# A decoder layer on one core: denominators of the cross-attention groups moved to the third quarter, and both ends rearranged

## What is computed

```python
x = x + attn(layernorm(x), w_qkv, b_qkv, w_dense, b_dense)              # causal, 16 heads of 32
x = x + xattn(layernorm(x), ctx, ctx, mask, Wq, bq, Wk, bk, Wv, bv, Wo, bo)
x = x + ffn(layernorm(x), Wg, bg, W1, b1, W2, b2)                       # argmax of 8 experts, gelu
# inside each attention
scores = einsum('bhqd,bhkd->bhqk', q, k) / sqrt(32)                     # masked
probs  = softmax(scores)
ctx    = einsum('bhqk,bhkd->bhqd', probs, v)
```

## Time and profile before

| What | Value |
|---|---|
| three runs | 1976.71, 1986.3, 1979.91 us; median 1979.91 |
| profiled execution, its own time | 1983.32 us |
| its span, and mean granted clock of PE | 1981.5 us, 0.978 |
| PE, DVE, ACT, POOL busy in the span | 1888.0, 1345.2, 1128.2, 971.7 us |
| cross-attention, 1000 to 1200 us: PE, DVE, ACT, POOL busy | 199.67, 133.37, 112.95, 101.50 us |
| the last attention group, 1575.5 to 1595.5 us: PE busy, granted clock | 17.81 us, 0.50 |
| start of the expert layer | 1613.73 us |

### The profile page before, as it was taken

One profiled execution on the slowest core, in us unless ns is written; L12 is line 12 of the kernel. 1 busy time (PEld: TensorE's weight loads), 2 busy tenths in 40 slices (PEclk: granted clock), 3 DMA queues, 4 the chain that ended last, 5 costly groups with the idle time before them and its releaser, 6 DMA issues. The chain is left out here.

```text
span 1981.5 us, 34914 instructions
## 1 busy us (share of the span) xinstructions
PE 1888.0 (95%) x10950; PEld 1327.1 (67%) x10950; DVE 1345.2 (68%) x2845; ACT 1128.2 (57%) x2164; POOL 971.7 (49%) x1144
## 2 busy tenths in 40 slices
PE   6899999999999999999999999999999875899997
PEld 4667777777777766666666666666666354798896
DVE  5567667676766676667675757576766357688886
ACT  3555555555555555555565556555655434677885
POOL 3445545545554555455554444555454433345553
PEclk9999999999999999999999999999999776999999
DMA  5454554645455574544344545445343446722220
GB/s 165 114 164 108 135 137 97 143 115 123 108 133 134 129 191 91 139 110 110 103 113 102 128 108 126 110 108 118 88 100 80 102 166 192 286 73 92 83 88 16
DMA packets 137659, 239.18 MB, mean 121 GB/s; under 512 B 31067, under 2 KB 32387, under 8 KB 137441
## 3 DMA queue, kind: packets, MB, share of 16 engines
q1 hardware_dynamic: 109184, 191.28, 35.5%
q0 software_dynamic: 21392, 45.37, 11.6%
q10 hardware_dynamic: 6928, 0.63, 0.2%
HBM read 114.84 MB, written 48.97 MB: 83 GB/s over the span
## 5 line engine op out<-in xcount | busy, mean ns | idle before, releaser
L543 ACT ACTIVATE attn_probs<-attn_sT 128x512 f32<-128x512 f32 (+3 forms) x1024 | 528.8, 518 | 475.8 <-PE attn_sT L840 472.4
L451 POOL TENSOR_TENSOR attn_probs<-attn_probs 128x512 f32<-128x512 f32 (+2 forms) x384 | 529.9, 1399 | 174.6 <-PE attn_o_ps L855 128.1
L648 DVE TENSOR_REDUCE attn_m_col<-attn_sS 128x1 f32<-128x512 f32 x512 | 342.6, 688 | 191.1 <-PE attn_sS L824 183.2
L840 PE MATMUL attn_sT<-attn_stack 98*128 98x512 f32 (+2 forms) x1024 | 389.4, 392 | 2.2 <-ACT attn_probs L543 2.2
L824 PE MATMUL attn_sS<-attn_stack 97*128 97x512 f32 (+2 forms) x1024 | 368.7, 370 | 12.6 <-DVE attn_m_col L648 3.2
L654 DVE CUSTOM_DVE_ANT_0 attn_sS<-attn_sS,attn_cT_low 128x128 f32<-128x128 f32 x496 | 241.2, 504 | 170.3 <-PE attn_sS L824 166.5
L840 PEld LDWEIGHTS attn_sT<-attn_stack 98*128 98x128 f32 x1024 | 189.0, 190 | 212.8 <-ACT attn_probs L543 135.1
L439 POOL TENSOR_SCALAR_AFFINE_SELECT attn_probs<-attn_probs 128x256 f32<-128x256 f32 x256 | 119.6, 468 | 350.8 <-ACT attn_probs L543 350.7
L855 PE MATMUL attn_o_ps<-attn_probs,attn_V 128*32 128x512 f32 (+3 forms) x2048 | 236.3, 533 | 6.1 <-ACT attn_probs L543 3.3
L824 PEld LDWEIGHTS attn_sS<-attn_stack 97*128 97x128 f32 x1024 | 193.5, 190 | 67.9 <-DVE attn_m_col L648 15.6
L804 PE MATMUL attn_pj<-attn_xT_high,attn_w_high 128*128 128x512 f32 x384 | 155.0, 404 | 2.6 <-DVE attn_xT_low L632 1.4
(11 more groups left out here) (198 smaller groups left out, 3689.4 us busy)
## 6 DMA issues: line engine op xcount, KB each, us to landing
attn_stack<-attn_stage SPq DMA_DIRECT2D x672, 128.0 KB, 2.3
attn_rows<-in_x_dram SPq DMA_DIRECT2D x64, 256.0 KB, 4.0
attn_rows<-x_after_self SPq DMA_DIRECT2D x64, 256.0 KB, 4.3
moe_w<-in_L_ffn_W_dram SPq DMA_DIRECT2D x16, 1024.0 KB, 15.0
attn_stack<-attn_stage POOLq DMA_DIRECT2D x96, 128.0 KB, 3.3
x_after_self<-attn_rows SPq DMA_DIRECT2D x32, 256.0 KB, 2.6
...
```

Source lines behind the costliest of these rows:

```text
L451: pool.tensor_tensor(total, total, tile_of(n, kb)[:, js, q0:S], ALU.add).then_inc(added, 1)
L543: act.activation(tile_of(n, kb)[:, j, q0:S], sT[:, i % 2, q0:S], ACT.Exp, scale=SCALE).then_inc(exp_done, 1)
L648: dve.tensor_reduce(to, sS[:, k % 2], AX_X, ALU.max).then_inc(s_free, 1)
L840: pe.matmul(sT[:, i % 2, q0:S], stack[0:ROW_MAX + 1, n % 2, 1, j, kb * P:(kb + 1) * P], stack[0:ROW_MAX + 1, n % 2, 0, j, q0:S], start=Tru ...
```

## The change

Five things change.

- **Denominators of late groups.** A late group is a cross group other than the first of its batch (`late`). There POOL adds the fourth key block to the sum tile as well, in two adds of 128x1024 at steps 14 and 15 (the second behind the stack head), and `sums` has only the four products with the sum tile. It runs at the end of step 3 of the next group instead of step 0 (`sums_q`). ACT takes the logarithm at step 4 and the inverse at step 5, DVE the three operations at steps 6 and 7.
- **Correction within PSUM**, in all groups: residual (extra times rec), then `correct_inverse` (extra becomes (extra + 2) times rec), then `divide` (o_sb times extra), at steps 2, 3, 4, or 6, 7, 7 behind a late group.
- **The start.** The first rows are normalised before the weights are split; the split goes in nine pieces, first the q and k columns of the four parts, then their v columns, then the dense weights; the heads 1 and 3 of group 0 are stacked by ACT's queue.
- **The end of attention.** The output of the last batch gets four banks of its own (both pj, both sS). Its chunks 0 to 2 are computed in steps 1 to 15 of group 63, only the four last chunks after the last group's output is split. The bias is added to the rows from step 12 of group 63. In group 63 the output of group 62 is split at steps 6 and 7.
- **The start of the expert layer.** POOL's memset of the row buffers moves behind the fourth batch's layernorm.

```diff
@@ -56,3 +56,3 @@
         what, of, t = (("v", b, 3), ("wo", b - 1, 1), ("wo", b - 1, 3), ("v", b + 1, 1))[g]
-        return (what, of, t) if in_batch(of) else None
+        return (what, of, t) if in_batch(of) and (what, of) != ("wo", NB_ALL - 1) else None
@@ -92,4 +92,10 @@
+    def late(n):
+        return is_cross(n) and n % G != 0
+
+    def sums_q(n):
+        return 3 if late(n) else 0
+
     def adds_before(n):
-        return 6 * n
+        return 6 * n + 2 * sum(late(m) for m in range(n))
@@ -127,3 +133,3 @@
             aux.append(turned_aux(n, q))
-        if q == 0 and in_groups(n - 1):
+        if q == sums_q(n - 1) and in_groups(n - 1):
             aux.append(("den", n - 1))
@@ -260,2 +267,4 @@
         tri_at = [flat.bitcast(BF16) for flat in (cT[1][:, 0, S // 2:S], rows[:, RING - 1, 0:S // 2])]
+        LAST_CHUNKS = {(NG - 1, q): (i % NB, i // NB) for i, q in enumerate((1, 2, 3, 4, 5, 6, 7, 8, 9, 11, 13, 15))}
+        last_bank = [pj[:, 0], pj[:, 1], sS[:, 0], sS[:, 1]]
         N_CONST = 15
@@ -321,2 +330,12 @@
+        N_SPLIT = 2 * KT + 1
+
+        def split_views(i):
+            if i == 2 * KT:
+                _, _, to, of = weight_views(KT)
+                return KT, to, of
+            _, _, to, of = weight_views(i % KT)
+            what = slice(0, 2) if i < KT else slice(2, 3)
+            return i % KT, [w[:, what] for w in to], of[:, what]
+
         def raw_dst(raw, src):
@@ -387,3 +406,3 @@
                 m, j = n + 2, q - J * (NB - 1)
-                if j >= 0 and in_groups(m) and not (is_cross(m) and j == POOL_HEAD):
+                if j >= 0 and in_groups(m) and not (is_cross(m) and j == POOL_HEAD) and not (m == 0 and j % 2):
                     wait_to_stack(sp, m, j)
@@ -404,2 +423,4 @@
             for t in range(NB):
+                store_row(LAST, t)
+            for t in range(NB):
                 sp.wait_ge(stored[t], 16 * NB_ALL)
@@ -449,2 +470,4 @@
                     pool.wait_ge(added, adds_before(n) + j1)
+                if kb == 3:
+                    pool.wait_ge(added, adds_before(n) + J + j1 // 2)
                 total = tile_of(n, 0)[:, js, q0:S]
@@ -453,3 +476,3 @@
             adds_at = {False: {6: ((1, 0, 1),), 8: ((1, 1, 2),), 10: ((1, 2, 3),), 11: ((1, 3, 4),), 12: ((2, 0, 2), (2, 2, 4))},
-                       True: {8: ((1, 0, 1), (1, 1, 2), (1, 2, 3), (1, 3, 4)), 12: ((2, 0, 2), (2, 2, 4))}}
+                       True: {8: ((1, 0, 1), (1, 1, 2), (1, 2, 3), (1, 3, 4)), 12: ((2, 0, 2), (2, 2, 4)), 14: ((3, 0, 2),), 15: ((3, 2, 4),)}}
@@ -481,5 +504,6 @@
                     stack_head(pool, n + 2, POOL_HEAD)
-                if in_groups(n) and q in adds_at[is_cross(n)]:
-                    for part in adds_at[is_cross(n)][q]:
-                        add_probs(n, *part)
+                if in_groups(n):
+                    for part in adds_at[is_cross(n)].get(q, ()):
+                        if part[0] < 3 or late(n):
+                            add_probs(n, *part)
                 u = finished(n - 1, 14) if q == 6 else finished(n, 0) if q == 7 else None
@@ -495,4 +519,4 @@
             def high_of_weights(i):
-                act.wait_ge(raw_loaded[i], 16)
-                _, _, (high, _), raw = weight_views(i)
+                part, (high, _), raw = split_views(i)
+                act.wait_ge(raw_loaded[part], 16)
                 act.copy(high, raw).then_inc(raw_high, 1)
@@ -571,3 +595,2 @@
-            high_of_weights(0)
             for t in range(NB):
@@ -575,4 +598,6 @@
             for n, q in steps:
+                if (n, q) == (-3, 14):
+                    high_of_weights(0)
                 if (n, q) == (-2, 1):
-                    for i in range(1, len(weights)):
+                    for i in range(1, N_SPLIT):
                         high_of_weights(i)
@@ -581,5 +606,6 @@
                     act.wait_ge(const_step, N_STEP)
-                    act.wait_ge(raw_done, len(weights))
+                    act.wait_ge(raw_done, N_SPLIT)
                 if q == 0 and in_groups(n - 1):
                     copy_output(n - 1)
+                if q == 0 and in_groups(n - 1) and not late(n - 1):
                     log_of_sums(n - 1)
@@ -587,3 +613,5 @@
                     exponent(n, q // J, q % J)
-                if q == 0 and in_groups(n - 1):
+                if q == 4 and in_groups(n - 1) and late(n - 1):
+                    log_of_sums(n - 1)
+                if q == (5 if late(n - 1) else 0) and in_groups(n - 1):
                     inverse_of_sums(n - 1)
@@ -599,2 +627,5 @@
                         high_of_rows(t)
+                if n == -2 and q in (13, 15):
+                    wait_to_stack(act, 0, q - 12)
+                    stack_head(act, 0, q - 12)
                 if q == 14 and in_groups(n + 1):
@@ -603,3 +634,3 @@
                                   m_neg[:].bitcast(F32)).then_inc(max_stacked, 16)
-                if q == (14 if n % G == 2 else 12) and in_groups(n - 1):
+                if q == (6 if n == NG - 1 else 14 if n % G == 2 else 12) and in_groups(n - 1):
                     high_of_output(n - 1)
@@ -669,12 +700,11 @@
+            def correct_inverse(n):
+                dve.wait_ge(refined, n + 1)
+                dve.scalar_tensor_tensor(out=extra[:], in0=extra[:], scalar=2.0, in1=rec[:], op0=ALU.add,
+                                         op1=ALU.mult).then_inc(o_scaled, 1)
+
             def divide(n):
                 dve.wait_ge(o_copied, n + 1)
-                dve.wait_ge(inverse_done, 2 * n + 2)
-                dve.tensor_tensor(o_sb[:], o_sb[:], rec[:], ALU.mult).then_inc(o_scaled, 1)
-
-            def refine(n):
-                dve.wait_ge(refined, n + 1)
                 dve.wait_ge(o_scaled, n + 1)
-                dve.scalar_tensor_tensor(out=o_sb[:], in0=extra[:], scalar=2.0, in1=o_sb[:], op0=ALU.add,
-                                         op1=ALU.mult).then_inc(o_divided, 1)
+                dve.tensor_tensor(o_sb[:], extra[:], o_sb[:], ALU.mult).then_inc(o_divided, 1)
                 dve.wait_ge(o_divided, n + 1)
@@ -688,2 +718,14 @@
+            def add_last_bias(t):
+                to = row_block(("r", LAST, t))
+                wait_row(dve, ("r", LAST, t))
+                wait_row(dve, BIAS_AT)
+                dve.tensor_tensor(to, to, row_block(BIAS_AT), ALU.add).then_inc(last_biased, 1)
+
+            def add_last_rows(t):
+                to = row_block(("r", LAST, t))
+                dve.wait_ge(last_biased, t + 1)
+                dve.wait_ge(last_full, t + 1)
+                dve.tensor_tensor(to, last_bank[t], to, ALU.add).then_inc(summed, 1)
+
             def add_rows(u):
@@ -692,6 +734,2 @@
                 wait_row(dve, ("r", b, t))
-                if b == LAST:
-                    wait_row(dve, BIAS_AT)
-                    dve.tensor_tensor(to, to, row_block(BIAS_AT), ALU.add).then_inc(last_biased, 1)
-                    dve.wait_ge(last_biased, t + 1)
                 wait_unit(dve, u)
@@ -708,6 +746,7 @@
                 row_stats(0, t)
-            low_of_weights(0)
             for n, q in steps:
+                if (n, q) == (-3, 15):
+                    low_of_weights(0)
                 if (n, q) == (-2, 1):
-                    for i in range(1, KT):
+                    for i in range(1, 2 * KT):
                         low_of_weights(i)
@@ -729,8 +768,8 @@
                         maximum(key)
-                if q == 2 and in_groups(n - 1):
-                    divide(n - 1)
-                if q == 3 and in_groups(n - 1):
+                if q == (6 if late(n - 1) else 2) and in_groups(n - 1):
                     residual_of_inverse(n - 1)
-                if q == 4 and in_groups(n - 1):
-                    refine(n - 1)
+                if q == (7 if late(n - 1) else 3) and in_groups(n - 1):
+                    correct_inverse(n - 1)
+                if q == (7 if late(n - 1) else 4) and in_groups(n - 1):
+                    divide(n - 1)
                 u = finished(n, q)
@@ -743,3 +782,3 @@
                     negate_max(n + 1)
-                if q == (15 if n % G == 2 else 13) and in_groups(n - 1):
+                if q == (7 if n == NG - 1 else 15 if n % G == 2 else 13) and in_groups(n - 1):
                     low_of_output(n - 1)
@@ -752,2 +791,6 @@
                     low_of_swap(*swap_at[before])
+                if n == NG - 1 and q >= NB * (J - 1):
+                    add_last_bias(q - NB * (J - 1))
+            for t in range(NB):
+                add_last_rows(t)
@@ -795,3 +838,3 @@
                     else:
-                        pe.wait_ge(raw_done, len(weights) if what == "wo" else 1 if u == units[0] else KT)
+                        pe.wait_ge(raw_done, N_SPLIT if what == "wo" else 2 * KT if what == "v" else 1 if u == units[0] else KT)
                 elif u == units[0]:
@@ -863,4 +906,4 @@
                 for j in range(J):
```

(30 more changed lines are left out.)

7 lines of the change are left out of this document (4 added, 3 removed).

## The result

The changed kernel takes 1974.55 us (median of 22 runs, 1968.54 to 1978.33), the kernel before 1977.82 (22 runs, 1973.18 to 1986.3): ratio 0.9976, 95% interval 0.9967 to 0.9986. That is 3.3 us by the medians and 2.8 to 6.5 by the interval, not the 16.4 forecast, and the time lies just above the range's upper end of 1974. One execution of the kernel before, in the series of E9 to E12, took 2320 us at a clock of 0.749; it is left out of every figure.

What follows compares the result with a forecast made beforehand. PE's own instructions bound the middle, the chain both ends; -10.7 + 2.1 - 3.0 - 0.3 - 4.5 = -16.4 us, from the median 1979.91 to 1963.5 us, range 1953 to 1974.

Steps and rivals of the forecast that it cites:

- Part 1: Late groups: two denominator sets leave the end (-1.71), one lone set comes (+1.20); -0.51 us each, -10.7 over 21.
- larger-gain rival: Late groups: a lone set costs only 0.87 us and DVE keeps up; about -27 in all, 1953 us; 13%.
- Part 2: Other engines in late groups: POOL's adds and ACT 0; DVE's three operations at steps 6 and 7 +2.1 us.
- POOL late for the sums: Next group's sums: POOL ready with 2.5 us to spare in the middle; in the last group some 1.6 us later.
- Part 4: End of attention: -0.3 us up to the denominators and -4.5 from the last oT to the last row sum.
- term for 12 products instead of 39: After the last oT: 12 products remain instead of 39; -3.7 to -6.2 us, taken as -4.5.
- Part 3: Start: ACT's split behind normalising and narrower low parts on DVE; -3.0 us, bounds -1.5 and -4.5.
- The memset: Expert layer's start: moving POOL's memset costs 0 to +2.4 us among the row statistics; taken as 0.
- Bunching: DVE's operations at steps 6 and 7 hold back score banks: +8 us (4%) or 27 more, slower (5%); 9%.
- port rival: Late groups: the output's low part on DVE held 1.5 us more, on PE's path; +31, 1995 us, slower; 4%.

Runs made afterwards that it cites:

- E9: Kernel before with the load of row block 2 moved from step 15 to step 13 of the batch's second group; 1977.36 us, ratio 0.9985.
- E12: Changed kernel with the edits of E7 and E8, and groups 62 and 63 not late; 1950.96 us, ratio 0.9860.
- E7: Changed kernel with the load of row block 2 moved from step 15 to step 13 of the batch's second group; 1965.12 us, ratio 0.9934.
- E10: Changed kernel with the edits of E7 and E8 together; 1957.02 us, ratio 0.9881.
- E2: Changed kernel with no group late, both ends and the correction within PSUM kept; 1970.02 us, ratio 0.9958.
- E1: Changed kernel run again without any edit, for a second profile; 1974.44 us, ratio 0.9978.
- E3: Changed kernel with DVE taking both maxima of step 0 ahead of the row sum; 1970.83 us, ratio 0.9963.
- E4: Changed kernel with group 63 not late; 1968.95 us, ratio 0.9954.
- E6: Changed kernel with groups 62 and 63 not late; 1967.44 us, ratio 0.9943.
- E8: Changed kernel with DVE's correction at step 8 and division at step 10 instead of 7, last group excepted; 1965.62 us, ratio 0.9932.
- E11: Changed kernel with the edits of E7 and E8, and group 63 not late; 1952.88 us, ratio 0.9865.

## Why the prediction was wrong, step by step

**What bounds it: held.** PE in the middle, the chain at the ends.

**Part 1, -10.7: held.** Away from the row waits a step takes nearly the same time in group after group, so the steps can be compared one by one. This is the third group of a batch, mean of seven, in us from one transposed score to the next:

| steps | before | E7 | E10 |
|---|---|---|---|
| 3 and 4 (the lone set) | 2.96 | 4.15 | 4.15 |
| 7 | 1.31 | 1.17 | 1.16 |
| 9 and 10 | 2.68 | 3.04 | 2.68 |
| 15 (the group's end) | 4.88 | 3.17 | 3.17 |
| all 16 | 25.39 | 25.07 | 24.71 |

The lone set costs 1.18 us, where I had 1.20, and the end gets 1.72 shorter, where I had 1.71: -0.54 a group, -11.3 in all. So the larger-gain rival's 0.87 for a lone set did not come. In E7, group 46:

```profile
1123.38 0.39 PE L867 MATMUL attn_sS<-attn_stack 97*128 97x512 f32 x1
1123.70 1.06 PE L907 MATMUL attn_extra<-attn_probs,attn_ones 128*32 128x512 f32 x8
1124.69 0.50 PE L883 MATMUL attn_sT<-attn_stack 98*128 98x512 f32 x1
```

**Part 2, DVE +2.1: mis-sized on both sides.** Steps 9 and 10 cost 0.38 us more a late group, 8.0 in all, where I took 0.1 (E10, with the operations apart, takes them back to the old length). The step that failed was the picture of the three operations "laid in one by one" against idle time on one side: steps 6 and 7 put two of them in a row ahead of maxima that were already due. What I put at nothing was the place that they leave: in the kernel before PE waited at step 7 for maxima held back by the same three operations at steps 2 to 4, and that wait is gone, 0.17 us a group, 3.7 in all. (In E2, where the operations are back at steps 2 to 4, step 7 takes 1.33 us again.) Group 46 before, at step 7, and in E7, at steps 9 and 10:

```profile
1136.03 0.19 PEld L824 LDWEIGHTS attn_sS<-attn_stack 97*128 97x128 f32 x1 [0.32 <-DVE attn_m_col L648]
```
```profile
1133.16 0.19 PEld L867 LDWEIGHTS attn_sS<-attn_stack 97*128 97x128 f32 x1 [0.39 <-DVE attn_m_col L679]
...
1133.76 0.19 PEld L867 LDWEIGHTS attn_sS<-attn_stack 97*128 97x128 f32 x1 [0.30 <-DVE attn_m_col L679]
```
A clean batch so came out 1.0 us shorter, where I had 1.2. E10 is 15.8 us shorter than the kernel before between groups 33 and 61, more than part 1 forecast, because the wait at step 7 is gone too, not because the sets cost less. The middle adds up: -11.3 for the sets, +8.0 at steps 9 and 10, -3.7 at step 7, -0.7 in small pieces, +5.0 for the rows below make -2.7, as measured.

**Part 2, what was not in the sum: the row.** This is one of the two steps that made the miss. I looked at what the moved work does to POOL's stack heads and bias loads, and saw DVE's row wait in group 62 only; that a shorter group makes SP's row load late for the third group of the other batches too stood at nothing, without a reason. The load and the heads ahead of it keep their time against the products of the group's end, but the group's end is 1.71 us shorter; so the row, which before landed 0.2 to 1.0 us ahead of the next group's start, now lands 0.4 to 0.7 after it, and in groups 42 and 54 3.3 and 1.6 after it. DVE's wait in all is the same as before, 15.6 us against 15.2, and now it is on PE's path. E7 prices it: 5.0 us between groups 33 and 61, and 9.3 by the medians with group 62, where the kernel before had that wait as well. Why it is just groups 42 and 54 stays open: ahead of group 42 one issue of a stack head took 1.3 to 1.9 us instead of 0.59 in each of six profiles with late sums and the load in its old place (after, E1, E3, E4, E6, E8), and the load 3.6 to 5.4 us to land, where in group 46 it took 2.9 to 3.6.

**POOL late for the sums: right in the middle,** where no product of L907 waited. **At the end** the wait was foreseen and priced at +1.6 us from the start of the group; it came to +2.7 (26.2 against 23.5). Of the 1.1 more, 0.9 are the last four adds, 10.42 us for four instead of 4 x 2.38, beside DVE's four bias additions, 7.96 us for four:

```profile
1572.44 7.96 DVE L723 TENSOR_TENSOR attn_rows<-attn_rows 128x512 f32<-128x512 f32 x4
```
```profile
1574.47 10.42 POOL L474 TENSOR_TENSOR attn_probs<-attn_probs 128x1024 f32<-128x1024 f32 x4 [0.82 <-ACT attn_probs L567]
```

**Part 4, -4.8: right against the wrong base,** the other step that made the miss. From group 61 to the last row sum the two profiles after are 4.0 and 3.4 us shorter than the one I worked from. But in that one the last group was at half clock; in three of five it is not, and against those (86.5) the changed kernel is 1.6 us slower: groups 61 and 62 take 1.8 us less, the last group 9.3 us more up to its denominators, and what follows 5.9 us less. I read the 0.50 of the earlier trace rows as what the kernel does, took its length as the thing to beat, and put the result on the median of all executions. The profiled execution's 3.4 us above the median could have warned me. The term for 12 products instead of 39, -4.5, held against its own base: from the last oT to the last row sum 5.48 us after, 9.94 before. There was luck in it: in the three profiles with a full-clock last group the same stretch took 11.5 us, 6.1 more than after.

**Part 3, -3.0: held** within what the profiles differ: 776.9 on average over the eleven profiles with the new start in the table, 779.7 over the six of the kernel before. The first score starts 4.0 us sooner on average, where I had 3. The memset I set at 0 within 0 to 2.4: the rest of the span is 1.0 us longer on average, 371.7 (E11 left out) against 370.7. Neither the start nor the memset was tried alone.

**The sum with what was measured:** start -2.8, middle -2.7, end +1.6 against the full-clock state and -3.7 against the other, rest +1.0: -2.9 or -8.2. The medians have -3.3, and 48 of 61 executions point to the first state. Of the 13.5 us between the forecast and -2.9, the end makes 6.4, the rows 5.0, the rest of the span 1.0, the remainder of the middle (DVE's operations above all) 0.9 and the start 0.2.

**The rivals.** None was the outcome. Bunching was there at its smaller price (0.38 us a group for its 8 us); nearly half of it was offset by the wait at step 7 that went. The port rival's hold was there more often than in the kernel before: L715 has a median of 1.26 us over the kernel (0.75 before), 2.48 at most, and 2.2 to 2.3 in each group ahead of one like 42. No price of it shows on the path: in E7 the same L715 still takes 2.25 and the row wait is gone, and steps 11 to 14 take 5.95 us before and in E7.

```profile
1007.60 2.25 DVE L715 SCALAR_TENSOR_TENSOR attn_oT_low<-attn_o_sb,attn_bias,attn_oT_high 128x512 fp32r<-128x512 f32 x1
```
This agrees with the rule of the Trainium skill cited in the prediction (SBUF — State Buffer, "SBUF: two separate sides"), and with the reason given there for not charging it.
